# A modulated layer-norm block on one core: the last six parts of wmod through two places, a norm a round earlier, row copies on ScalarE

## The reference

```
mod = silu(c) @ wmod               # (4, 1024) @ (1024, 6 * 1024)
sa, ca, ga, sb, cb, gb = six rows of 1024 per batch
ga, gb: magnitude at least 0.25, sign kept
h = layernorm(x) * (1 + ca) + sa
x = x + ga * (h @ (weight * block_mask).T)          # 1024 x 1024
h = layernorm(x) * (1 + cb) + sb
x = x + gb * ((silu(h @ w1.T) * (h @ w2.T)) @ w3.T) # w1, w2, w3: 4-bit codes, scales, 1024 x 2752
```

## Time and profile before

| | |
|---|---|
| median of 3 runs | 1575.8 us (1574.83 to 1576.04) |
| profiled execution | 1575.16 us, span 1573.4 us |
| TensorE (PE) busy | 1541.3 us, 98% |
| VectorE (DVE) busy | 1033.3 us, 66% |
| ScalarE (ACT) busy | 986.9 us, 63% |
| granted TensorE clock, mean of the span | 0.996 of 2.4 GHz |
| chain that ended last | PE 93%, DVE 3%, DMA 2%, ACT 1%, issue 1% |

### The profile page before, as it was taken

One profiled execution on the slowest core, in us unless ns is written; L12 is line 12 of the kernel. 1 busy time (PEld: TensorE's weight loads), 2 busy tenths in 40 slices (PEclk: granted clock), 3 DMA queues, 4 the chain that ended last, 5 costly groups with the idle time before them and its releaser, 6 DMA issues.

```text
span 1573.4 us, 19155 instructions
## 1 busy us (share of the span) xinstructions
PE 1541.3 (98%) x7200; PEld 1271.2 (81%) x7200; DVE 1033.3 (66%) x1494; ACT 986.9 (63%) x1282; POOL 5.5 (0%) x10
## 2 busy tenths in 40 slices
PE   5889999999999999999999999999999999999999
PEld 3678888888888888888888888888888888888887
DVE  5787786554655455547676666666875758856994
ACT  3465676998888888883898988886333433333220
POOL 0000000000000000000000000000000000000000
PEclk9999999999999999999999999999999999999999
DMA  9965422465545455443778787786787968947973
GB/s 368 370 242 191 173 93 107 170 201 193 194 138 195 160 174 181 149 142 101 252 233 240 207 253 207 210 247 184 251 301 262 339 199 297 345 161 269 398 277 123
DMA packets 170139, 345.97 MB, mean 220 GB/s; under 512 B 14752, under 2 KB 65344, under 8 KB 170048
## 3 DMA queue, kind: packets, MB, share of 16 engines
q1 hardware_dynamic: 170048, 344.76, 64.9%
HBM read 249.77 MB, written 94.93 MB: 219 GB/s over the span
## 4 chain that ended last, share of the span: by engine, by line
PE 93%; DVE 3%; DMA 2%; ACT 1%; issue 1%; SPq 0%; ACTq 0%; DVEq 0%
PE ps L1895 10%; PE ps L1894 10%; PE ps L1893 10%; PE ps L1967 9%; PE ps L1966 9%; PE ps L1968 9%; PE ps L1904 9%; PE ps L1906 9%; PE ps L1905 9%; PE ps L1811 3%; PE ps L1813 3%; PE ps L1812 3%; DMA wmod<-wmod 2%; PE ps L1768 2%; PE ps L1751 1%; ACT modulated L887 1%
## 5 line engine op out<-in xcount | busy, mean ns | idle before, releaser
L842 ACT ACTIVATE w_raw<-w_raw 128x1024 f32<-128x1024 f32 x287 | 304.7, 1062 | 9.1
L1893 PE MATMUL ps<-ffn_in_hi,w_hi 128*128 128x512 f32 x688 | 268.6, 390 | 0.0
L1895 PE MATMUL ps<-ffn_in_hi,w_lo 128*128 128x512 f32 x688 | 267.8, 389 | 0.0
L1894 PE MATMUL ps<-ffn_in_lo,w_hi 128*128 128x512 f32 x688 | 267.7, 389 | 0.0
L1966 PE MATMUL ps<-t_hi,s_hi 128*128 128x512 f32 x616 | 239.6, 389 | 0.0
L1967 PE MATMUL ps<-t_lo,s_hi 128*128 128x512 f32 x616 | 239.6, 389 | 0.0
L1968 PE MATMUL ps<-t_hi,s_lo 128*128 128x512 f32 x616 | 239.6, 389 | 0.0
L1904 PE MATMUL ps<-x_m_hi,stream_hi 128*128 128x512 f32 x604 | 235.0, 389 | 0.0
L1905 PE MATMUL ps<-x_m_lo,stream_hi 128*128 128x512 f32 x604 | 235.0, 389 | 0.0
L1906 PE MATMUL ps<-x_m_hi,stream_lo 128*128 128x512 f32 x604 | 235.0, 389 | 0.0
L1088 ACT ACTIVATE s_hi<-s_raw 128x1408 fp32r<-128x1408 f32 x56 | 77.4, 1383 | 239.4 <-DVE s_raw L1603 191.2
(11 more groups left out here) (137 smaller groups left out, 2082.2 us busy)
## 6 DMA issues: line engine op xcount, KB each, us to landing
s_raw<-h_d SPq DMA_DIRECT2D x96, 704.0 KB, 5.6
stream_raw<-t_d SPq DMA_DIRECT2D x150, 256.0 KB, 3.4
t_d<-combined SPq DMA_DIRECT2D x106, 256.0 KB, 2.6
wmod<-wmod SPq DMA_DIRECT2D x12, 2048.0 KB, 15.4
t_raw<-w_d SPq DMA_DIRECT2D x88, 256.0 KB, 6.1
w_codes<-w12q SPq DMA_DIRECT2D x41, 512.0 KB, 5.3
h_d<-h_tile SPq DMA_DIRECT2D x44, 256.0 KB, 2.4
h_d<-up_c SPq DMA_DIRECT2D x44, 256.0 KB, 3.3
```

Source lines behind the costliest of these rows:

```text
L842: act.activation(RAWF[r], RAWF[r] if j else RQ[r][:], ACT.Prelu, bias=bias, scale=sign, alpha=slope).then_inc(line_ready, 1)
L1893: pe.matmul(acc, RH[r][:, k, :], HH[:, b, k, :], start=(k == 0), stop=False)
L1894: pe.matmul(acc, RH[r][:, k, :], HL[:, b, k, :], start=False, stop=False)
L1895: last = pe.matmul(acc, RL[r][:, k, :], HH[:, b, k, :], start=False, stop=(k == C - 1))
```

## The change

Parts 0 to 5 of wmod keep the three places; parts 6 to 11 use places 0 and 1 alone. Part 5's place (64 KB) then holds x of tile 6 and a second attention gate (`GA[1]`, tiles 4 to 7), both loaded ahead of the loop; the gate of tiles 4 to 7 is no longer loaded in round 3. Part 8 is issued in round 1 instead of ahead of the loop, parts 9, 10, 11 in rounds 2, 6, 7 (before 2, 4, 6). Tile 6's sums, factors, root and norm move from round 4 to round 3, the norm ahead of the second four decoding lines. Rows 3 and 4 are copied by ScalarE in rounds 2 and 6 (before by VectorE in 3 and 6). TensorE's order is unchanged.

```diff
-    XE = [at(f"x_extra_{i}", [D], F32, kb) for i, kb in enumerate((ST + 28, 88))]
-    EXTRA = (TPB, TPB + 1)
+    XE = [at(f"x_extra_{i}", [D], F32, kb) for i, kb in enumerate((ST + 28, 88, 64))]
+    EXTRA = (TPB, TPB + 1, TPB + 2)
...
-    GA = at("attn_gate", [D], F32, ST + 32)
+    GA = [at(f"attn_gate_{i}", [D], F32, kb) for i, kb in enumerate((ST + 32, 68))]
+
+    def ga_of(t):
+        return GA[1 if t // TPB == 1 else 0]
...
+    MOD_PARTS = 6
+
+    def wmod_slot(j):
+        return j % 3 if j < MOD_PARTS else j % 2
+
+    def wmod_loads(j):
+        return 16 * sum(wmod_slot(k) == wmod_slot(j) for k in range(j + 1))
...
             def load_wmod(j):
+                i = wmod_slot(j)
                 if j >= 3:
-                    sp.wait_ge(wmod_used, j - 2)
+                    sp.wait_ge(wmod_used, max(k for k in range(j) if wmod_slot(k) == i) + 1)
...
             store_gate(0)
             sp.wait_ge(gate_stored, 64)
-            load_ga(batch_of(0))
-            load_wmod(8)
+            load_ga(0)
+            sp.wait_ge(wmod_used, MOD_PARTS)
+            load_x(EXTRA[2])
+            load_ga(TPB)
...
-                if k == TPB - 1 and t < TILES - 1:
-                    load_ga(batch_of(t + 1))
+                if k == TPB - 1 and TPB < t < TILES - 1:
+                    load_ga(t + 1)
...
-                if t in (2, 4, 6):
-                    load_wmod({2: 9, 4: 10, 6: 11}[t])
+                if t in (1, 2, 6, 7):
+                    load_wmod({1: 8, 2: 9, 6: 10, 7: 11}[t])
...
             def copy_rows(m):
                 act.wait_ge(wmod_used, 2 * (m + 1))
                 if m:
-                    act.wait_ge(mod_turned, m)
+                    act.wait_ge(mod_turned, m if m < 3 else m - 1)
                 for q in range(4):
-                    ins = act.activation(quarter_of(VEC[0], q), quarter_in_psum(m, q), ACT.Copy)
+                    ins = act.activation(quarter_of(VEC[m // 3], q), quarter_in_psum(m, q), ACT.Copy)
...
-                if t + 2 < TILES and t not in (1, 2, 3):
+                if t == 3:
+                    start1(6)
+                elif t + 2 < TILES and t not in (1, 2, 4):
                     start1(t + 2)
+                if t in (2, 6):
+                    copy_rows(t // 4 + 3)
                 if t in (2, 3, 6, 7):
                     early_lines(t // 4, NL // 2 * (t % 2), NL // 2 * (t % 2 + 1))
...
-                if 3 < t < TILES - 2:
+                if t == 3:
+                    ln1_sums(6)
+                elif 4 < t < TILES - 2:
                     ln1_sums(t + 2)
...
-                if 3 < t < TILES - 2:
+                if t == 3:
+                    ln1_factors(6)
+                elif 4 < t < TILES - 2:
                     ln1_factors(t + 2)
...
-                if t in (3, 6):
-                    copy_rows(t // 3 + 2)
-                elif t in (5, 8):
+                if t in (5, 8):
                     read_mod(t // 3 + 2)
...
             def modulation(j):
 
                 m, half = j // 2, j % 2
-                pe.wait_ge(wmod_loaded[j % 3], 16 * (j // 3 + 1))
+                pe.wait_ge(wmod_loaded[wmod_slot(j)], wmod_loads(j))
```

More of the change, by code:

```diff
@@ L202, in adaln_kernel @@
     sem = nc.alloc_semaphore
-    c_loaded, ga_loaded, gb_loaded = sem("c_loaded"), sem("ga_loaded"), sem("gb_loaded")
+    c_loaded, gb_loaded = sem("c_loaded"), sem("gb_loaded")
+    ga_loaded = [sem(f"ga_loaded_{i}") for i in range(2)]
     gate_stored = sem("gate_stored")
@@ L435, in load_wmod @@
             def load_wmod(j):
+                i = wmod_slot(j)
                 if j >= 3:
-                    sp.wait_ge(wmod_used, j - 2)
+                    sp.wait_ge(wmod_used, max(k for k in range(j) if wmod_slot(k) == i) + 1)
                 m, half = j // 2, j % 2
-                sp.dma_start(WM[j % 3][:], wmod_v[:, 4 * half:4 * half + 4, m * D:(m + 1) * D]).then_inc(wmod_loaded[j % 3], 16)
+                sp.dma_start(WM[i][:], wmod_v[:, 4 * half:4 * half + 4, m * D:(m + 1) * D]).then_inc(wmod_loaded[i], 16)
             def load_codes(n, w):
@@ L509, in store_gate, with load_ga @@
                     sp.dma_start(gates_d[g][:, q * QUARTER:(q + 1) * QUARTER], MAG[32 * q:32 * q + BATCH, :]).then_inc(gate_stored, 16)
-            def load_ga(b):
-                sp.dma_start(GA[:], gates_d[0, b].partition_broadcast(P)).then_inc(ga_loaded, 16)
+            def load_ga(t):
+                sp.dma_start(ga_of(t)[:], gates_d[0, batch_of(t)].partition_broadcast(P)).then_inc(ga_loaded[1 if t // TPB == 1 else 0], 16)
             store_gate(0)
             sp.wait_ge(gate_stored, 64)
-            load_ga(batch_of(0))
-            load_wmod(8)
+            load_ga(0)
+            sp.wait_ge(wmod_used, MOD_PARTS)
+            load_x(EXTRA[2])
+            load_ga(TPB)
             def load_normed(d):
@@ L1192, in read_mod @@
                     dve.tensor_scalar(MODS[ln][:, :, s * C:(s + 1) * C], src, float(s), None, ALU.add).then_inc(mod_read, 1)
[L1194 to L1200, removed]
             def gate(g):
@@ L1282, in low_part2 @@
                 if e == 0:
-                    dve.wait_ge(x2_stored[1], 16 * (EXTRA[1] // TPB + 1))
+                    for i in (1, 2):
+                        dve.wait_ge(x2_stored[i], 16 * (EXTRA[i] // TPB + 1))
                 dve.tensor_tensor(HL[:, b, :, k * P:(k + 1) * P], HM[1][:],
@@ L1299, in residual_sum @@
                 if k == 0:
-                    dve.wait_ge(ga_loaded, 16 * (t // TPB + 1))
+                    dve.wait_ge(ga_loaded[1 if t // TPB == 1 else 0], 16 * max(1, t // TPB))
                 if 2 <= t < HALF_TILES + 2:
@@ L1306, in residual_sum @@
                     dve.wait_ge(gated, t + 1)
-                    dve.tensor_tensor(two, two, GA[:], ALU.mult).then_inc(early_gated, 1)
+                    dve.tensor_tensor(two, two, ga_of(t)[:], ALU.mult).then_inc(early_gated, 1)
                     dve.wait_ge(early_gated, t + 1)
                 else:
-                    dve.tensor_tensor(two, attn_in_psum(t), GA[:], ALU.mult).then_inc(gated, 1)
+                    dve.tensor_tensor(two, attn_in_psum(t), ga_of(t)[:], ALU.mult).then_inc(gated, 1)
                     dve.wait_ge(gated, t + 1)
@@ L1751, in modulation @@
                         last = pe.matmul(ps[32 * q:32 * (q + 1), MOD_BANK[m], 0:QUARTER], SC[:, 4 * half + cc, :],
-                                         WM[j % 3][:, cc, q * QUARTER:(q + 1) * QUARTER],
+                                         WM[wmod_slot(j)][:, cc, q * QUARTER:(q + 1) * QUARTER],
                                          start=(half == 0 and cc == 0), stop=(half == 1 and cc == 3))
```

## The result

The changed kernel takes 1585.22 us (1584.42 to 1586.31, 6 runs), the kernel before 1575.77 (1574.83 to 1576.15, 6 runs): ratio 1.0061, interval 1.005 to 1.0072, so 9.4 us slower. The profiled execution has a span of 1583.8 us against 1573.4, +10.4.

A forecast was written before the change was run, and what follows sets the result against it. TensorE, busy 98% of the span, was taken to bound the kernel. P (+0.4) plus 9.6 for part 11 gave +10.0 us on the profiled 1575.16, so 1585.2, as median 1585.8; own range 1583 to 1588, forecast range 1579 to 1588.5 (75%).

The forecast's parts named there:

- Round 3: Tile 6's turn: the wait for its norm is replaced by one for tile 5's modulation; turn at 114.7, was 117.25.
- Rounds 4 and 5: VectorE runs late, reads row 3 from 130.14; TensorE idles 0.6 to 2.0 us, starts part 8 at 130.4.
- the second gap: TensorE's idle time before part 8, 0.6 to 2.0 us; whether it lowers the clock was left open.
- P: The shift at tile 7 against the kernel before: +0.4 us (-0.4 to +1.3).
- The middle between 0 and 1.67: Low-clock cost assumed for the gap before part 8: 0.8 us.
- Round 6: ScalarE's copy of row 4 passes 1.44 us through to its read; TensorE idles 1.0 us before part 10.
- Part 11: Issued at 170.9, landing at 180.9, wanted at 174.1: TensorE idles 6.8 us; tile 10's turn +9.6 us.
- Rival A: At tile 6's turn the stall of 6.2 us goes and nothing comes back: faster, 1569.6 us; 4%.
- B: The stall at tile 6 goes wholly (-6.2), only part 11 is late (+9.6): 1579.2 us; 12%.
- the 6.2 us: TensorE's stall at tile 6's turn, 4.49 plus 1.67 for the low clock: all the change can win.
- C: Part 11 doesn't matter, the early part comes back as worked out, +1.4: about 1577 us; 4%.
- D: Part 11 takes as long as with a crowded queue, or lead is lost further on: 1590 and above; 5%.

The follow-up runs named there:

- the copies alone: The kernel before with only rows 3 and 4 copied by ScalarE in rounds 2 and 6: 1577.89 us, ratio 1.0012.
- parts in time: The changed kernel with parts 10 and 11 issued in rounds 5 and 6 instead of 6 and 7: 1576.31 us, ratio 1.0005.
- part 11 late alone: The kernel before with part 11 issued in round 7 instead of 6, three places kept: 1585.68 us, ratio 1.0061.
- the lines alone: On top of parts in time, ScalarE's round 3 reordered: two decoding lines, tile 6's root, two lines, tile 6's norm: 1576.71 us, ratio 1.0006.
- part 9 in round 1: On top of the lines alone, part 9 issued in round 1 behind part 8 instead of in round 2: 1577.38 us, ratio 1.0007.
- reads forward: On top of parts in time, VectorE's reads of rows 3 and 4 moved right behind the residual sum in rounds 5 and 8: 1575.23 us, ratio 0.9995.

## Why the prediction was right

It said 1585.8 and the median is 1585.2; of +10.0 us against the profiled execution, the trace has +10.4. By its steps:

- Round 3 was worked out to little over 0.1 us: norm at 106.37 (106.29), lines 107.52 (107.45), modulation 111.74 (111.79), turn 114.7 (114.83), product 117.0 (117.09). That the lines stand in the way was argued from order and is shown by the kernel that moved them: the wait went.
- Rounds 4 and 5: the read of row 3 at 130.14 (130.18), part 8 at 130.4 (130.51). The low clock cost the product of tile 5 close to its top value of 1.7 (12.8 us from 117.09 to the last matmul's end, against 11.2 for tile 8's product in the kernel before, taken the same way), and so the second gap was 0.62 and the clock stayed up: P was -0.3 and not +0.4. The middle between 0 and 1.67 was a guess, and it was the smaller gap that came.
- Round 6: 1.0 us before part 10 was 1.10; confirmed by the copies alone (1.1).
- Part 11: wanted at 174.1 + P (174.1), issued at 170.9 + P (170.74), 10.0 to landing (10.8; 9.9 to 10.9 in the four other profiles with it late), low clock 1.67 (1.7). +9.6 became +10.7 from tile 7 to tile 10. By the estimate of 6.8 us from the Trainium skill's page "DMA: Bandwidth & Descriptors", section "Anatomy of one DMA", which is for a DMA by itself on the GpSimd path, the time would have been 3 to 4 us less. The trace disagrees for a load behind others in SyncE's queue.

So the mechanism held at each step, but that the sum came within 0.4 us of the trace is in part luck: P came 0.7 lower than the sum had it, and part 11 landed 0.8 later, and the two cancel. The 10.0 was also drawn from a mixed lot. Of the five transfers of the earlier trace rows only three, those issued at 105.03, 127.63 and 156.43, had x and the normed result ahead of them, and they took 10.6, 9.9 and 10.5 us; the 8.0 at the low end of the range and a 9.7 were of parts 7 and 8, which had not. And the price of the low clock was taken from a product that ends at a turn; from tile 8's turn to part 10, at full clock and ending at a part, it is 12.01 (159.20 to 171.21) and not 11.92, so 1.58 and not 1.67. Its count of the waits is one short, which changed nothing: two of TensorE's waits lie behind 60 us, the second of 0.5 us, at 269.01.

Rival A and B needed the 6.2 us to stay won; the parts in time alone (1576.3) exclude both. C, part 11 without effect, falls with part 11 late alone (+9.6). D (1590 and above) did not come: part 11 took 10.8 us, and no execution was over 1586.45.

What the prediction didn't see: x of tile 7. It said that VectorE was the next limit after the lines, which held for the changed kernel only because VectorE was late there. With the lines out of the way a load was next, and my forecasts for the lines alone and with part 9 in round 1 missed by the whole gain.

## What to carry to other kernels

On an engine that issues in order, a transfer starts when everything ahead of it has been released: taking a place away from a ring of buffers cost nothing here by itself (1576.3), but ask in which round each issue lands, and subtract a measured landing time from its use. A step that is moved earlier on one engine and waits there moves everything behind it later; look at what stands behind it before looking at what it feeds. When one stall is covered by several chains of nearly equal length, repairs look worthless one by one and must be tried together.

## What the runs showed of the hardware that was not expected

- Where a gap puts the low clock varies. After the same gap of 2.14 us ahead of tile 6's turn, the fall came at 113 to 114 us in one profile (changed kernel), 115 to 116 in another (reads forward) and after 116 in a third (parts in time), and the product of tile 5 behind it, which starts at 117.1 or 117.2 us, took 12.8, 13.6 and 12.6 us to the last matmul's end, against 11.2 for tile 8's product in the kernel before. A cost of 1.4 to 2.4 us thus hangs on a gap of the same length.
- A gap of 1.1 us before part 10 did not lower the clock in any of the eight profiles that have it (part 10 in 1.93 us, or both parts in 3.66).
- 2 MB loads behind two transfers of 512 KB took 9.9 to 10.9 us from issue to landing. The store of tile 3's result (512 KB, issued at 106.6 to 110.0 us, DMA share about 1.0) took 8.5 to 10.5 us, and 8.6 in the kernel before too; stores elsewhere in that kernel took 2.6 at best.
